# Attention and routing: the products with the values first in TensorE's iteration, a tile's addition first in VectorE's

## What is computed

```python
x = x + _L0_conv_ref(_gn(x), ...)        # strided depthwise convolutions, 8 query heads, softmax
t = _to_tokens(x)                        # 16 images of 1024 tokens of 128 values
t = t + _L1_attn_ref(_ln_t(t), WQ, WK, WV)
t = t + _L1_ffn_ref(_ln_t(t), router_w, w1, w2, w3)   # 8 experts, each token goes to 2
```

```python
W = einsum('bqd,bkd->bqk', Q, K) / scale
M = where(W == 0, 0, tril)
x_exp = exp(W - max(W, axis=-1)) * M
A = x_exp / (sum(x_exp, axis=-1) + 1e-9)
return einsum('bqk,bkd->bqd', A, V)
```

## Time and profile before

| | |
|---|---|
| median of 3 runs | 2069.62 us (2067.84 to 2073.09) |
| the profiled execution's time | 2068.77 us |
| its span in the trace | 2067.0 us |
| TensorE, VectorE, GpSimd, ScalarE busy over the span | 90%, 66%, 65%, 48% |

### The profile page before, as it was taken

The page is one execution under the profiler, slowest core; times in us unless marked ns, Lnnn a source line. Parts: engine busy times, 40 slices in busy tenths (PEclk is TensorE's granted clock), DMA queues, the critical chain, the costliest instruction groups (busy, mean ns, idle before and its releaser), DMA issues. The chain is left out here.

```text
span 2067.0 us, 45504 instructions
## 1 busy us (share of the span) xinstructions
PE 1862.9 (90%) x11956; PEld 1396.3 (68%) x11956; DVE 1356.7 (66%) x3732; ACT 985.3 (48%) x2210; POOL 1349.0 (65%) x1623
## 2 busy tenths in 40 slices
PE   3999999999999988988889898984399999999997
PEld 2665666656666546655666566653399999999997
DVE  3777777777777757888778777875444444444443
ACT  0555555555555544444344343431255555555554
POOL 1767677677676635455554555556488888788887
PEclk8999999999999999999999999997699999999999
DMA  6333333232333221111111111111244454444544
GB/s 208 90 75 78 74 77 78 74 77 72 76 78 76 53 78 56 32 45 37 40 38 42 38 40 37 45 35 51 63 64 65 63 66 64 62 66 63 64 65 51
DMA packets 175444, 132.08 MB, mean 64 GB/s; under 512 B 33437, under 2 KB 164933, under 8 KB 175301
## 3 DMA queue, kind: packets, MB, share of 16 engines
q0 software_dynamic: 55808, 52.50, 15.9%
q1 hardware_dynamic: 118341, 77.16, 14.2%
q10 hardware_dynamic: 1152, 0.54, 0.1%
HBM read 31.47 MB, written 46.71 MB: 38 GB/s over the span
## 5 line engine op out<-in xcount | busy, mean ns | idle before, releaser
L1773 POOL DMA_INDIRECT out<-f_y,f_rows x272 | 423.8, 1558 | 45.7 <-POOL f_waited L1771 41.9
L496 DVE TENSOR_REDUCE neg_max<-s_bank 128x2 f32<-128x512 f32 x512 | 328.3, 682 | 65.9 <-PE s_bank L788 63.4
L1836 DVE SCALAR_TENSOR_TENSOR f_hidden<-f_silu,f_rows,f_h_bank 128x341 f32<-128x341 f32 x272 | 155.4, 571 | 305.5 <-ACT f_silu L1805 282.8
L623 ACT ACTIVATE probsT<-st_bank 128x512 f32<-128x512 f32 x512 | 277.3, 597 | 71.5 <-PE st_bank L806 71.3
L1205 POOL DMA_INDIRECT routed<-a_rows,a_target_idx x256 | 252.3, 985 | 68.8 <-issue 68.8
L1582 PE MATMUL a_score_bank<-t_eT,t_gT 128*128 128x512 f32 x512 | 254.2, 621 | 1.2 <-DVE a_val L1249 1.2
L379 POOL TENSOR_TENSOR odd_sums<-probsT 128x512 f32<-128x512 f32 x128 | 162.1, 1275 | 129.3 <-ACT probsT L623 78.7
L1884 PE MATMUL f_y_bank<-w,f_hiddenT 114*128 (+1 forms) x1632 | 230.3, 277 | 1.3 <-ACT f_hiddenT L1797 1.3
L1215 POOL TENSOR_TENSOR a_causal_probs<-a_causal_probs,a_tril 128x128 f32<-128x128 f32 x128 | 58.3, 456 | 248.0 <-DVE a_causal_probs L1301 240.7
L1884 PEld LDWEIGHTS f_y_bank<-w,f_hiddenT 114*128 114x128 f32 (+1 forms) x1632 | 203.1, 191 | 8.3 <-issue 1.8
L1797 ACT ACTIVATE f_hiddenT<-f_hT_bank 114x384 f32<-114x384 f32 x272 | 133.6, 491 | 142.2 <-PE f_hT_bank L1875 80.7
(11 more groups left out here) (224 smaller groups left out, 3752.6 us busy)
## 6 DMA issues: line engine op xcount, KB each, us to landing
q_stack<-q_high SPq DMA_DIRECT2D x512, 64.0 KB, 2.1
f_rows<-routed SPq DMA_DIRECT2D x272, 66.0 KB
q_stack<-q_low POOLq DMA_DIRECT2D x256, 64.0 KB, 2.3
out<-X SPq DMA_DIRECT2D x16, 512.0 KB, 3.2
X<-in_x SPq DMA_DIRECT2D x1, 6144.0 KB, 21.3
out<-f_y,f_rows POOLq DMA_INDIRECT x272
q_stack<-max_rows SPq DMA_DIRECT2D x256, 4.0 KB
routed<-a_rows,a_target_idx POOLq DMA_INDIRECT x256
```

What stands on the lines that cost most here:

```text
L496: dve.tensor_reduce(neg_max[:, i % 2, CT * j:CT * (j + 1)], s_bank[h % 2][:], AX_X, ALU.max, negate=True).then_inc(max_ready, 1)
L623: act.activation(probsT[:, i % 4, c, lt, :], st_bank[lt][:], ACT.Exp).then_inc(exp_done, 1)
L1773: pool.indirect_dma_start(out=out, out_offset=bass.IndirectOffsetOnAxis(ap=rows[:, i, TOKEN:TOKEN + 1].bitcast(I32), axis=0), in_=y[:, i, ...
```

## The change

In TensorE's `period` V(i-3) goes from the end of the iteration to its start, ahead of T(i-2) and S(i). In VectorE's, A(i-3) goes from between the longer task and K(i) to the start, ahead of X(i). Nothing is added or removed, and no wait's count is changed.

```diff
                 def period(b, slot):          # VectorE
                     for i in range(TT):
+                        summed = tile(b, slot, i - 3)
+                        if has(summed[0]):
+                            add(*summed)
                         if has(b):
                             tile_max(b, i)
...
                             targets(b - 2, slot)
                             gates(b - 2, slot)
-                        summed = tile(b, slot, i - 3)
-                        if has(summed[0]):
-                            add(*summed)
                         if has(b):
                             mask(b, i)
 
                 def period(b, slot):          # TensorE
                     for i in range(TT):
+                        summed = tile(b, slot, i - 3)
+                        if has(summed[0]):
+                            values(*summed, b)
                         image, _, j = tile(b, slot, i - 2)
                         if has(image):
                             turn(b, j, image * TT + j)
...
                         for kind, back in PREPARED[i]:
                             if has(b + back):
                                 prepare(b, slot, kind)
-                        summed = tile(b, slot, i - 3)
-                        if has(summed[0]):
-                            values(*summed, b)
```

## The result

| | before | after |
|---|---|---|
| median of 4 runs on one chip | 2070.32 us | 2050.41 us (2048.24 to 2051.73) |
| ratio | | 0.9902, interval 0.9885 to 0.9920 |
| the profiled execution's span | 2067.0 us | 2050.0 us |

The change makes the kernel 19.9 us faster where 9.2 were forecast. In the spans, 17.0 us are to be accounted for: the thirteen periods from K(3) of image 2 to K(3) of image 15 took 543.2 us and take 526.9 (-16.3, forecast -6.1); the stretch from the last mask to the gate of the last scatters is 4.8 shorter (forecast -4); the start of the stage up to K(3) of image 2 is 0.6 shorter (forecast +1.2); the last image up to its K(7) is 0.2 longer, and the stages in front and behind, which are the same code, took 2.2 and 2.4 us more. So the ends came out as forecast within 2 us, and the miss is the period: 41.78 became 40.53, not 41.3.

What follows compares the result with a forecast made beforehand. Neither TensorE nor VectorE was full; each waited for the other in turn. 13.7 periods at 0.47 us gave 6.4, plus 4 at the end, less 1.2 for image 1: 9.2 us, median 2060.4, range 2049 to 2077.

Steps and rivals of the forecast that it cites:

- the four stretches: Parts of a period, by iterations, for each of which the prediction named the engine or wait that comes last.
- iteration 5: VectorE: A(2) moves into the wait for GpSimd's power, so K(5) ends earlier: -0.76 us a period.
- iteration 2: VectorE: A(7) moves into the wait for the power; iterations 1 and 2 were booked together at -0.77 us.
- iteration 6: VectorE: nothing lies between X(6) and K(6), so all of E(6) is waited for: +0.76 us.
- iteration 7: VectorE: A(4) no longer waits for V(4) behind l, but K(7) waits for E(7): -0.3 us.
- the tail: After the last image: V(6) precedes c, A(7) comes sooner and the last scatters start earlier: 4 us gained.
- iteration 0: TensorE's stream from r: X(0) comes 1.08 us later, less 0.76 of VectorE work behind it: +0.3 in all.
- I keep the 1.0 between them.: The 1.0 us between S(0)'s end by recorded starts, 9.8 after r, and X(0), 10.83 after r, was kept unchanged.
- rival 1: The clock stays up without the idle stretch before r: 2055 us, up to 2044; chance 0.13.
- Image 1: At the start, V(7) precedes T(0) and S(2) under the slow clock: K(2) and all after 1.2 us late.
- (2): Rival: TensorE's chain from r to S(2), with 0.5 us of slack, eats the gain: 2067 to 2070 us; chance 0.27.
- (3): Rival: new idle places before V(4), V(7), V(0) bring slow-clock stretches: 2072 to 2096 us; chance 0.14.

Runs made afterwards that it cites:

- before_add2_again: Kernel before with A(2) alone moved ahead of the normalisation, into VectorE's wait for the power, run beside a trace of the kernel before: ratio 0.9976.
- after_busy5: Changed kernel with one extra 512-column product in TensorE's idle time before V(3), its result overwritten: 2052.95 us, ratio 0.9883.
- values_first: Kernel before with TensorE's half of the change alone, VectorE as before: 2494.2 us, ratio 1.193.
- after_old0: Changed kernel with iteration 0 alone put back in its old order on both engines: 2128.0 us, ratio 1.028.
- before_unrolled_busy2: Kernel before with its loop written out and two extra 512-column products in each of TensorE's idle stretches, before V(2) and before r: 2063.7 us, ratio 0.9898.
- before_again: Kernel before, unchanged, traced on the chip where before_add2_again ran: ratio 1.0002.
- before_busy_both: Kernel before with one unread 512-column product in each of TensorE's idle stretches, before V(2) and before r: ratio 1.0003.
- before_add2: Kernel before with A(2) alone moved ahead of the normalisation, into VectorE's wait for the power: 2072.2 us, ratio 0.9925.
- before_unrolled_add2: Kernel before with its loop written out and A(2) alone moved ahead of the normalisation: 2059.2 us, ratio 0.985.
- after_unrolled: Changed kernel with the loop over pairs of images written out: 2039.9 us, ratio 0.9829 to the kernel before.
- before_unrolled: Kernel before with the loop over pairs of images written out: 2074.8 us, ratio 0.9935.
- before_unrolled_busy: Kernel before with its loop written out and one extra 512-column product in each of TensorE's idle stretches, before V(2) and before r: 2064.3 us, ratio 0.9886.
- before_unrolled_short_v: Kernel before with its loop written out and V(3) and V(4) stopped after two products each: 2057.0 us, ratio 0.9849.
- after_unrolled_busy5: Changed kernel with its loop written out and one extra 512-column product in the idle stretch before V(3): 2043.4 us, ratio 0.9796.

## Why the prediction was wrong

**Right, with their sizes.** The reading of the four stretches; that the idle 2.15 us before V(2) would cost nothing and reappear before V(3); iteration 5 (-0.72 for -0.76) and iteration 2 (-0.81 for -0.77), both by a wait for the power that fell to 0.4; iteration 6, where K(6) came to wait for E(6), which took +0.63 of it back (forecast +0.76); iteration 7 (-0.33 for -0.3); the tail (-4.8 for -4); image 0 costing nothing. before_add2_again confirms the step of iteration 5 by itself (0.71). after_busy5 bounds what the recorded slow clock costs after the change, 0.13 a period.

**The step that failed** is in iteration 0: "I keep the 1.0 between them." I measured 10.83 from r to X(0), found 9.8 by the recorded starts and took the difference to be a fixed part of the stream, to which V(5) in place of V(3) and the wait for A(3) were then added: 10.83 became 11.9. Measured, X(0) comes 10.26 after r in the loop and 10.87 in the written-out images. The two additions are there in full: in the written-out images the modelled end of S(0) is 10.84 after r instead of 9.8. The 1.0 is not; the gap is 0.03 to 0.14. In the written-out images the time from r to X(0) therefore hardly changed (10.7 and 10.8 before, 10.9 and 11.0 after). From the end of K(3) to X(0) it is 21.08 before and 21.45 after in the loop's images without the jump, +0.37 instead of the +1.08 that I booked: r starts 0.94 later, behind the recorded slow stretch, so V(4) has no A(3) to wait for and the stream from r to the end of S(0) is 0.26 longer instead of 1.08, and the gap is 0.84 shorter. In the mean over all images iteration 0 is 0.64 a period better than forecast, or 8.3 of the 10.2 us by which the periods were missed. The rest is 0.13 of iteration 6, 0.08 of iteration 1 and small amounts of both signs. In the text the possibility stood as the end of rival 1 ("if the 1.0 in the stream from r goes too, up to 2044"), with 0.13 in all for rival 1; it should have been the main uncertainty, with bounds of 0 and 1.0 on the term, since a distance without a known cause has no reason to survive a change of order. Two sums of the rivals do not come out: from 2055.3 a further 1.0 a period leads to 2041.6, not 2044, and three slow stretches in two images, at 1.25 and 2.95 an image, come to 2084, not 2077. Neither enters the forecast.

**A second misreading** did not move the sum: I read the earlier trace rows, X(0) waiting until 11.5 after r at a full recorded clock, as an unrecorded slow clock. By the runs above it is the jump back of the loop, in every second image. The chance of rival 1 was argued down with this row, which says nothing about the clock. Where the prediction says "The trace agrees", it rests on the same reading, and these rows do not support it.

**Image 1** was forecast 1.2 late; K(3) of image 2 came 0.6 early. I had let V(7) delay S(2) there by its slow-clock length and had not sized the gains of the same kind as in later images.

**The rivals.** The stream did not eat the gain (2): X(2) and X(3) wait for nothing in the loop. The new idle places were not followed by costly slow stretches (3). values_first and after_old0 show where a slower result would have come from: an addition that is late, not the clock.

**What the gap is stays open.** Shown is: with one and the same kernel and TensorE's recorded starts alike to 0.01 us up to S(0), it was 1.97 at the upper level and 0.49 at the lower; it stays when all idle time is filled (0.96 to 2.48 in before_unrolled_busy2); it falls to 0.2 with 0.7 us less work in front of it; the recorded clock is full meanwhile. In the undisturbed images, without the jump, without a recorded slow stretch and not behind the loop's end:

| kernel | the kernel before beside it | gap at X(0) |
|---|---|---|
| before, before_again, before_busy_both | 2070 to 2074 | 0.8 to 1.0 |
| before_add2_again | 2072 | 0.4 to 0.5 |
| before_add2, before_unrolled_add2 | 2090, 2087 | 0.6 to 3.3 |
| after, after_busy5, after_unrolled | 2070 to 2074 | 0.03 to 0.14 |
| before_unrolled | 2090 | 2.4 (once 1.0, once 1.7) |
| before_unrolled_busy, before_unrolled_busy2 | 2087, 2086 | 0.25 to 2.5 |
| before_unrolled_short_v | 2087 | 0.04 to 0.22 (once 1.0) |
| after_unrolled_busy5 | 2086 | 0.04 to 1.5 |

Every gap above 1.2 in such an image was measured at the upper level (behind the loop's end the kernel before has 1.6 at the lower one). The level and the program both bear on it, and the runs do not separate them: no trace of the kernel before, of the change or of after_unrolled was taken at the upper level, none of before_unrolled at the lower. The values at the upper level come in steps of about 0.7 (0.2, 1.0, 1.7, 2.4, and 0.04, 0.8, 1.5). That points to a slowing of TensorE in a long dense stretch which neither its recorded starts nor the recorded clock show. That it is the clock is only argued. The Trainium skill, page "TensorE: Matmul & The Clock Gate", section "What's actually happening", says in its caveats that the recorded clock events have been seen to be unreliable. The windows above with a recorded 1.00 and gaps of 1.5 to 2.4 us agree with it, but would look the same if another cause held the stream back. A run that would separate them, with the end of each product observed by another engine, was not made.

Why the changed order has no gap at the lower level is open in the same way. The idle stretch before V(3) does not explain it, since after_busy5 has no gap with part of this stretch filled.

## What to carry over

When an engine is seen to start later than the modelled end of what it waits for, and nothing names the reason, that distance is not a constant of the stream: put it into the range with zero as an end. Two engines that hand work back and forth in a written-out order must be moved together, and each iteration's first instruction must find its partner's result ahead of the partner's long task; half of such a change cost 6% and 19% here. Look at the images on both sides of a loop's jump separately before averaging them. And when the unchanged kernel itself comes at two levels, take a trace of it beside each experiment: without one, a period of one level set against a period of the other gives the level's effect to the edit.

## What the runs showed of the hardware

- The jump back of the loop costs VectorE 1.83 us ahead of its first instruction and another 0.62 a little later, once for two images; in the changed kernel an image with the jump takes 1.6 to 1.8 us longer. Writing the loop out took 1.06 off the mean period (40.53 to 39.47), ratio 0.9829 against 0.9902 for the change alone, and 0.65% off the kernel before.
- Filling TensorE's idle time raised the mean recorded clock and gave little: 0.966 to 0.973 with a ratio of 1.0003 (before_busy_both), 0.968 to 0.977 with 0.9883 against 0.9902 (after_busy5). Written out, half of the idle time filled gave 0.9886 and all of it 0.9898 against 0.9935, at recorded clocks of 0.975, 0.974 and 0.965. A higher recorded clock was not in step with a shorter time.
- With 0.7 us less work on TensorE the next result came 2.9 us sooner (before_unrolled_short_v against before_unrolled).
- VectorE started 1.97 us behind the modelled end of the product that it waited for, and 0.49 in another execution of the same kernel, with the same recorded starts and a recorded full clock (before_add2, before_add2_again).
- The same edit measured 0.9925 and 0.9976 on two chips, with intervals that do not touch; the unchanged kernel's median was 2070 to 2074 us beside some runs and 2086 to 2090 beside others.
